# Cross-attention, float32, one core: the key mask leaves TensorE's score product and is added on GpSimd to the loaded scores

## The reference, cut to what matters

```python
a = layer_norm(audio_kv) * ln_gamma + ln_beta          # (8, 64, 1024)
Q = (hidden_states @ Wq.T)  -> (8, 16 heads, 1024, 64)
K = (a @ Wk.T)              -> (8, 16 heads, 64, 64)
V = (a @ Wv.T)
scores = einsum('bhtd,bhsd->bhts', Q, K) * 64 ** -0.5
scores = where(mask[:, None, None, :], scores, -inf)   # mask: (8, 64), one row per batch
out = einsum('bhts,bhsd->bhtd', softmax(scores), V)
return hidden_states + tanh(gate) * (out @ Wo.T)
```

## Time and profile before

| | |
|---|---|
| median of 3 runs | 1564.25 us (1563.99 to 1564.56) |
| the profiled execution's own time | 1560.93 us |
| its span | 1559.2 us |
| granted TensorE clock over the span | 0.999 |
| TensorE busy (matmul) | 1531.3 us, 98% |
| VectorE busy | 1128.9 us, 72% |
| ScalarE busy | 872.8 us, 56% |
| GpSimd busy | 356.1 us, 23% |

### The profile page before, as it was taken

One profiled execution on the slowest core, in us unless ns is written; L12 is line 12 of the kernel. 1 busy time (PEld: TensorE's weight loads), 2 busy tenths in 40 slices (PEclk: granted clock), 3 DMA queues, 4 the chain that ended last, 5 costly groups with the idle time before them and its releaser, 6 DMA issues.

```text
span 1559.2 us, 20380 instructions
## 1 busy us (share of the span) xinstructions
PE 1531.3 (98%) x7104; PEld 1245.8 (80%) x7104; DVE 1128.9 (72%) x1356; ACT 872.8 (56%) x1874; POOL 356.1 (23%) x254
## 2 busy tenths in 40 slices
PE   7999899999999999999999999999999999999998
PEld 5666778888888888887887888888888888888887
DVE  6445888787878787879857777777777777777643
ACT  3556445454545454547766666666666666666521
POOL 5333000000000000001233344432344333444320
PEclk9999999999999999999999999999999999999999
DMA  7799765656565656556689344553445533445321
GB/s 251 222 364 392 275 215 178 210 202 222 178 220 187 211 182 216 190 188 184 202 292 294 115 136 142 157 157 114 125 125 168 169 123 120 123 145 167 109 93 69
DMA packets 225077, 289.77 MB, mean 186 GB/s; under 512 B 28240, under 2 KB 112336, under 8 KB 224976
## 3 DMA queue, kind: packets, MB, share of 16 engines
q1 hardware_dynamic: 224976, 288.48, 56.6%
HBM read 168.89 MB, written 116.39 MB: 183 GB/s over the span
## 4 chain that ended last, share of the span: by engine, by line
PE 90%; DMA 4%; DVE 3%; issue 1%; SPq 1%; ACT 0%; POOL 0%; DVEq 0%; ACTq 0%
PE banks L1036 28%; PE banks L1038 28%; PE banks L1037 28%; PE banks L1104 4%; PE banks L1065 3%; DMA wo_split_scratch<-wo_ring 1%; DMA xq<-x_t 1%; DMA m_scratch<-m_stage 1%; DVE parts L878 1%; DMA s_scratch<-c_out 1%; DVE a_sum L939 1%; DVE a_ring L872 1%; ACT a_ring L684 0%; PE banks L1160 0%; DMA c_out<-x 0%
## 5 line engine op out<-in xcount | busy, mean ns | idle before, releaser
L1036 PE MATMUL banks<-parts,a_ring 128*128 128x512 f32 x1792 | 711.6, 397 | 5.8 <-DVE a_ring L872 3.6
L1038 PE MATMUL banks<-parts,a_ring 128*128 128x512 f32 x1792 | 700.1, 391 | 0.0
L1037 PE MATMUL banks<-parts,a_ring 128*128 128x512 f32 x1792 | 698.9, 390 | 0.0
L1036 PEld LDWEIGHTS banks<-parts,a_ring 128*128 128x128 f32 x1792 | 336.9, 188 | 75.3 <-DVE a_ring L872 5.9
L1038 PEld LDWEIGHTS banks<-parts,a_ring 128*128 128x128 f32 x1792 | 336.8, 188 | 72.2
L1037 PEld LDWEIGHTS banks<-parts,a_ring 128*128 128x128 f32 x1792 | 337.4, 188 | 66.7
L961 DVE TENSOR_TENSOR c_out<-banks,c_out 128x1024 f32<-128x1024 f32 x160 | 195.5, 1222 | 147.9 <-PE banks L1038 142.6
L732 ACT ACTIVATE probs<-probs,neg_max 128x64 f32<-128x64 f32 x1024 | 259.1, 342 | 1.7 <-DVE neg_max L966 1.7
L684 ACT CAST a_ring<-a_sum 128x1024 fp32r<-128x1024 f32 x128 | 134.3, 1049 | 219.4 <-PE banks L1038 199.6
L597 POOL TENSOR_TENSOR probs<-probs,row_rec 128x512 f32<-128x512 f32 x128 | 134.5, 1051 | 479.7 <-DVE row_rec L975 479.7
L872 DVE TENSOR_TENSOR a_ring<-a_sum,a_ring 128x1024 fp32r<-128x1024 f32 x128 | 180.3, 1409 | 79.4 <-ACT a_ring L684 79.4
(11 more groups left out here) (75 smaller groups left out, 1354.4 us busy)
## 6 DMA issues: line engine op xcount, KB each, us to landing
xq<-x_t SPq DMA_DIRECT2D x32, 1024.0 KB, 6.8
s_scratch<-c_out SPq DMA_DIRECT2D x64, 512.0 KB, 3.1
probs<-s_scratch SPq DMA_DIRECT2D x128, 256.0 KB, 4.0
c_out<-x SPq DMA_DIRECT2D x64, 512.0 KB, 4.5
out<-c_out SPq DMA_DIRECT2D x64, 512.0 KB, 3.1
b_raw<-m_scratch SPq DMA_DIRECT2D x29, 1024.0 KB, 6.7
m_scratch<-m_stage SPq DMA_DIRECT2D x16, 1792.0 KB, 13.9
wo_split_scratch<-wo_ring SPq DMA_DIRECT2D x56, 256.0 KB, 5.7
```

The lines of the kernel that those rows point to most:

```text
L1036: pe.matmul(to, wl, mh, start=first, stop=False, skip_group_check=joined)
L1037: pe.matmul(to, wh, ml, start=False, stop=False, skip_group_check=joined)
L1038: return pe.matmul(to, wh, mh, start=False, stop=last, skip_group_check=joined)
```

## The change

The mask no longer goes through TensorE. `mask_f`, the mask of all batches as (mask - 1) * 2^100 in all partitions, which was made in the setup anyway and lay under `mask_mov`, gets memory of its own. For each unit GpSimd adds the batch's row of `mask_f`, broadcast over the 8 groups, to the loaded scores in place, and the row maximum waits for that (`mask_made`) where it waited for the load. `ones_row`, `mask_mov`, their clearing, `make_mask` and the 32 matmuls of L1160 go. The place of the addition in GpSimd's order is one slot ahead of the unit's row maximum (`soft_slot(u) == z + 1`).

```diff
-        ones_row = sb("ones_row", [P, P], F32R)
-        mask_mov = sb("mask_mov", [P, NC, S], F32R)
-        mask_off = nc.sbuf_base - NC * S * 4
-        mask_f = nc.alloc_sbuf_tensor_at("mask_f", [P, B, S], F32, offset=mask_off)
+        mask_f = sb("mask_f", [P, B, S])
...
-            nc.gpsimd.memset(ones_row[:].bitcast(F32), 0.0).then_inc(rows_zeroed, 1)
...
-            pool.wait_ge(rows_zeroed, 1)
-            nc.gpsimd.memset(ones_row[0:1, :].bitcast(F32), 1.0).then_inc(rows_zeroed, 1)
...
+            def add_mask(u):
+                pr = prob(u).rearrange("p (g s) -> p g s", s=S)
+                if u == 0:
+                    pool.wait_ge(mask_step, 1)
+                pool.wait_ge(s_in[u % PROBS], 16 * (u // PROBS + 1))
+                src = mask_f[:, u // 16:u // 16 + 1, :].to_broadcast([P, 8, S])
+                nc.gpsimd.tensor_tensor(pr, pr, src, ALU.add).then_inc(mask_made, 1)
...
-                for u in units(soft_slot, 2 * s - SUM):
-                    normalise(u)
-                for u in units(soft_slot, 2 * s + 1 - SUM):
-                    normalise(u)
+                for z in (2 * s, 2 * s + 1):
+                    for u in units(soft_slot, z + 1):
+                        add_mask(u)
+                    for u in units(soft_slot, z - SUM):
+                        normalise(u)
...
-            def make_mask(rnd):
-                wait(dve, item_done, 2 * (14 * (rnd - 1) + 8))
-                src = mask_u8[0:1, rnd:rnd + 1, :].to_broadcast([1, NC, S])
-                nc.vector.tensor_scalar(mask_mov[0:1], src, -1.0, BIG, ALU.add, ALU.mult).then_inc(mask_made, 1)
...
             def row_max(u):
-                dve.wait_ge(s_in[u % PROBS], 16 * (u // PROBS + 1))
+                dve.wait_ge(mask_made, u + 1)
                 wait(dve, exp_done, u - 1)
...
-            nc.vector.memset(mask_mov[:].bitcast(F32), 0.0).then_inc(rows_zeroed, 1)
-            dve.wait_ge(rows_zeroed, 3)
-            make_mask(0)
...
-                if s % 14 == 9 and s // 14 + 1 < B:
-                    make_mask(s // 14 + 1)
...
-                    if k == P1 and n < ROUNDS:
-                        pe.wait_ge(mask_made, rnd + 1)
...
-                if k == P1 and n < ROUNDS:
-                    pe.matmul(to, ones_row[:], mask_mov[:].rearrange("p h s -> p (h s)"), start=True, stop=False,
-                              skip_group_check=True)
-                    opens = False
```

More of the change, by code:

```diff
@@ L113, in xattn_kernel @@
         ident_made = sem("ident_made")
-        rows_zeroed = sem("rows_zeroed")
         mask_step = sem("mask_step")
```

## The result

The change makes the kernel slower: 1567.05 us against 1564.12 us, the medians of 16 runs each, a ratio of 1.0018 with a 95% interval of 1.0011 to 1.0025. That is 2.9 us where 2.1 us faster was forecast.

A forecast was written before the change was run, and what follows sets the result against it. The prediction took TensorE as the bound almost everywhere, except where late VectorE low parts hold it up. Its terms, 5.5 - 3.1 - 0.3 = 2.1 us faster, gave 1562.1 us, with a range of 1560.0 to 1566.5 us.

The forecast's parts named there:

- The gain, 5.5 us: Scores stage: removing the mask matmuls gains 24 x 0.23 = 5.5 us, from 12 of the 16 rounds.
- Rounds 3 and 9: Scores stage, late matmuls at 307.43 and 540.13 us: the chain behind them doesn't get shorter, so no gain counted.
- Round 15: Scores stage: one of the 12 rounds whose removed matmuls were counted in the 5.5 us gained.
- The additions' 1.1 us: Each of the 128 GpSimd additions was taken at 1.1 us, between 1.04 and 1.27; GpSimd about 32% busy.
- Output stage 0 us: Output stage: two additions behind GpSimd's last sum of a round make nothing late, 0 us for 15 rounds.
- The third rival: Output stage: GpSimd keeps the ports across queued operations, 0.6 us per round, 9 us, 1571 us; chance 0.1.
- Steps 1 to 5 of the head: Softmax head, 717 to 742 us: additions delay VectorE's maximum and low parts, TensorE starts later at 740; 3.1 us lost.
- step 6: Behind the late matmul of 740 us: units 6, 7 and 8 meet a full VectorE; 0.3 us lost (0 to 2.2).
- step 1: Softmax head, from 720.88 us: unit 2's addition stands behind the clearing of `v_diag`; unit 2's maximum is 3.1 us late.
- the head costs more: Rival at the softmax head: more additions hit VectorE, 5.7 us and up to 2 more, 1564.4 to 1566.5; chance 0.2.

The follow-up runs named there:

- e1: The change without any mask: no matmuls and no additions; 1559.81 us against 1565.72 for the kernel before, ratio 0.9962.
- e10: The change itself measured once more; 1567.14 us against 1562.52 for the kernel before, ratio 1.0031.
- e8: The change with each addition replaced by a same-shape GpSimd operation on its own tile, which no maximum awaits; 1566.65 us against 1563.50 for the kernel before.
- e9: The change with each addition replaced by a one-column clearing that the row maximum still awaits; 1556.58 us against 1563.50 for the kernel before.
- e5: The change with unit 2's addition moved ahead of the clearing of v_diag; 1565.71 us against 1563.50 for the kernel before, ratio 1.0008.
- e6: The change with the softmax pipeline 3 slots closer to the transposes; 1559.04 us against 1563.50 for the kernel before, ratio 0.9971.
- e11: The change with the softmax pipeline 2 slots closer to the transposes; 1561.50 us against 1562.52 for the kernel before, ratio 0.9993.

## Why the prediction was wrong, point by point

- **What bounds the kernel:** right. TensorE, except behind late low parts.
- **The gain, 5.5 us:** 5.9 us by e1; a tenth low. Two errors partly cancel. Rounds 3 and 9, which I set to nothing, kept theirs in this trace: up to step 96 there were 6.1 us, and 26 matmuls (two in each of rounds 1 to 13) of 0.227 us make 5.9. Round 15, which I counted, loses its gain in the wait at 820 us (e1). That rounds 3 and 9 kept it is partly luck: their waits were to grow by 0.46 us each, and the second shrank (0.85 to 0.73 us); in e10's trace of the same kernel it is 1.47 us.
- **The additions' 1.1 us:** 1.28 us. I chose between 1.04 and 1.27 and was low; the weight split, a full two-input operation, was the right row. With the waits for the ports GpSimd is busy for 35%, not 32%.
- **Output stage 0 us:** right from step 116 on, 713.8 us in the traces; its first rounds belong to the head's loss. The third rival (ports held across two additions) did not happen: in round 22 VectorE gets in between GpSimd's sum and the two additions behind it (GpSimd's rows, then VectorE's).

```profile
1109.21 2.41 POOL L584 TENSOR_TENSOR a_sum<-xq 128x1024 f32<-128x1024 f32 x1
1111.59 3.54 POOL L592 TENSOR_TENSOR probs<-probs,mask_f 128x512 f32<-128x512 f32 x2
...
1110.61 2.10 DVE L869 TENSOR_TENSOR a_ring<-a_sum,a_ring 128x1024 fp32r<-128x1024 f32 x1 [0.21 <-ACT a_ring L686]
```

- **Steps 1 to 5 of the head:** the idle of unit 2's maximum (3.1, measured 3.16) and the late matmul of 740 us (4.7, measured 4.36) came out; 3.1 us lost stand against 4.2 between steps 96 and 102, of which 0.9 lie in step 96, which these steps leave out. The weight I gave the idle was not right: e8 has none and the same loss, e9 has 1.95 us of it and no loss, and by e5 it is 0.9 of the 4.2 us. It was mostly the turns at the ports, of which I had put unit 4's in the wrong gap. That the size came out all the same is in part luck.
- **The step that failed: step 6, "I add 0.3 us (0 to 2.2)", with the list of places that it closes.** From step 102 to 116 the change lost 3.8 us, not 0.3: 2.2 us in step 102, which ran mostly at the lower clock after the long wait (8.28 us against 6.10); 0.8 us at 781 us; 1.1 us at 824 us, where an addition lengthens the low part (2.00 us for 1.22) directly behind VectorE's wait for a late transfer of x (3.98 us before, 4.17 after); less 0.2 in the other steps, among them what round 15's matmuls give. The other missing place is ahead of step 1: 0.9 us in step 96, where units 0 and 1 meet a low part as soon as their loads land (I had looked at VectorE from 717 us on, not at 703). So 3.4 us lost in all were forecast, and 4.2 + 3.8 = 8.0 measured.
- **The range** ended at 1566.5, 0.6 us short of the median. The rival "the head costs more" had the right place and sign, but its worst case lacked the clock.

What stays open: the clock's part is read from traces, not isolated, and it differs between executions of one kernel. Behind the same wait of 4.4 us the clock was at 0.57 from 739 to 745 us in the change's trace and at 0.72 in e10's, where step 102 is 1.6 us longer than before, not 2.2. But e10 has a second slow stretch behind its wait of 2.32 us at 826 us, where the change's trace, behind 1.94 us, has none (columns as above):

```profile
826.00:830.00 4.00, 4.00 (x14) 3.21 (x14) 3.96 (x5) 0.59 (x1) 3.65 (x4) 0.57 1.03 309
```

It makes step 114 1.5 us longer. e5 and e8 have it at the same place (waits of 2.40 and 2.41 us; a clock of 0.66 and 0.57 in that window), so the trace of the change shown here is one of the cheaper ones. All waits of 2.2 us and more from step 2 on were followed by a slow stretch; of the shorter ones, 1.16 (before), 1.57 and 1.61 us (e1) were not, and 1.78 us (e6) was, for some 3 us. A wait's length alone does not decide it: every trace has one of 1.79 us near 202 us, and only e11's is followed by a lower clock (0.66 from 203 to 208 us). How much of the 2.2 us would remain at full clock no run tells. e10's ratio, 1.0031, has an interval that overlaps the first result's (1.0019 to 1.0042, 1.0011 to 1.0025), so the two don't contradict each other.

## What to carry to other kernels

When work moves from TensorE to GpSimd, price it first as port time of VectorE wherever VectorE is full, and only then as the wait of whoever reads the result (here 0.9 of 4.2 us up to step 102). Look for all places where the new operation becomes ready, from the landing of its first load on, and add the clock to a wait of TensorE of 2 us or more (here 1.5 to 2.5 us by which the step behind it was longer). A pipeline's start that overlaps another stage's last work can be moved by its slack before the edit is judged: here three slots turned 2.9 us lost into 4.5 us gained.

## What the runs showed of the hardware that I had not expected

- GpSimd and VectorE take turns at the ports even when both have work ready: GpSimd's operation, asked for at 727.78, took 2.27 us where 1.28 is usual, so by its length it started as VectorE's ended, at about 728.8, in front of VectorE's next at 728.82. Each then needs 2.3 us for 1.2. In the earlier trace rows GpSimd had waited through a run of VectorE's instead; the difference may be the wait for its own result that VectorE's next operation has here, which was not tried.
- A wait of TensorE's costs more than its length: 4.36 us of idle were followed by some 5 us in which matmuls came 0.43 us apart, at a granted clock of 0.57, and that step was 2.2 us longer.
- Two executions of the same kernel can pay the clock at different places: 38.6 us from step 96 to 102 in both traces of the change, but 99.0 and 100.9 us from there to step 116.
